# Layer two's queries and keys: one product per quarter batch, spread to row groups through device memory

## The reference, cut to what matters

```python
Q = split_heads(X @ W_q.T)
K = split_heads(X @ W_k.T)
Q1, Q2 = (Q[..., :dh], Q[..., dh:])
K1, K2 = (K[..., :dh], K[..., dh:])
A1 = jnp.einsum('bhqd,bhkd->bhqk', Q1, K1) * scaling
A2 = jnp.einsum('bhqd,bhkd->bhqk', Q2, K2) * scaling
attn = jax.nn.softmax(A1, -1) - lam * jax.nn.softmax(A2, -1)
```

## Time and profile before

| what | value |
|---|---|
| median of 3 runs | 1149.87 us (1148.67 to 1150.07) |
| the profiled execution's own time | 1149.82 us |
| its span in the trace | 1148.1 us |
| PE busy | 915.2 us, 80% |
| DVE busy | 842.1 us, 73% |
| ACT busy | 578.9 us, 50% |
| POOL busy | 435.1 us, 38% |
| layer two in the span | from 461.4 to 1148.1 |

### The profile page before, as it was taken

How to read it: one execution, slowest core, us unless ns; L and a number is a source line. 1 busy time by engine, 2 the same in 40 slices (tenths; PEclk the granted TensorE clock), 3 DMA queues, 4 the chain that set the end, 5 groups by cost and what they waited for, 6 DMA issues and landing times.

```text
span 1148.1 us, 17547 instructions
## 1 busy us (share of the span) xinstructions
PE 915.2 (80%) x5805; PEld 564.9 (49%) x5805; DVE 842.1 (73%) x1990; ACT 578.9 (50%) x1401; POOL 435.1 (38%) x623
## 2 busy tenths in 40 slices
PE   7643086797697998888788888888999998987793
PEld 5322034444344556554343453344566665665692
DVE  4587989969999934587667767778677888835674
ACT  4535244354345343455554455544667765684372
POOL 0302353453283514123435224434532427833422
PEclk9867596898799999999988898999999999999797
DMA  7500000001000000100000000002145503462473
GB/s 205 180 0 1 1 0 1 1 0 42 1 1 1 1 1 1 56 1 1 2 1 1 1 1 1 1 1 97 57 125 157 161 17 106 123 203 61 148 247 101
DMA packets 54314, 60.41 MB, mean 53 GB/s; under 512 B 6208, under 2 KB 40656, under 8 KB 54224
## 3 DMA queue, kind: packets, MB, share of 16 engines
q1 hardware_dynamic: 52176, 55.10, 15.8%
q0 software_dynamic: 2048, 4.20, 1.3%
HBM read 46.05 MB, written 13.24 MB: 52 GB/s over the span
## 4 chain that ended last, share of the span: by engine, by line
PE 33%; DVE 11%; ACT 6%; issue 4%; POOL 3%; DMA 1%; POOLq 0%; ACTq 0%; SPq 0%; DVEq 0%
PE banks L857 8%; PE banks L1018 5%; PE banks L933 4%; DVE MX L1532 3%; PE banks L951 3%; PE banks L992 2%; POOL oms L2037 2%; PE banks L888 2%; ACT PT L1852 2%; PE banks L958 1%; ACT yh L1784 1%; PE banks L899 1%; PE banks L1005 1%; PE banks L1030 1%; DVE sil L1481 1%
## 5 line engine op out<-in xcount | busy, mean ns | idle before, releaser
L1532 DVE TENSOR_REDUCE MX<-banks 128x4 f32<-128x512 f32 (+2 forms) x192 | 199.4, 1043 | 51.4 <-PE banks L992 50.8
L1852 ACT ACTIVATE PT<-banks 128x768 f32<-128x768 f32 (+1 forms) x192 | 168.0, 879 | 88.3 <-PE banks L951 87.8
L2014 POOL TENSOR_SCALAR_AFFINE_SELECT PT<-PT 128x256 f32<-128x256 f32 x256 | 105.5, 428 | 174.0 <-ACT PT L1852 173.6
L1737 ACT ACTIVATE T<-Sb,GM 128x32 f32<-128x32 f32 x128 | 45.2, 353 | 122.8 <-DVE Sb L1407 122.6
L958 PE MATMUL banks<-KS,QS 32*128 32x512 f32 (+3 forms) x512 | 90.4, 399 | 13.2 <-DVE MX L1532 11.4
L1018 PE MATMUL banks<-PT,VA 128*17 128x512 f32 (+3 forms) x1024 | 91.8, 455 | 9.0 <-POOL PT L2014 5.3
L951 PE MATMUL banks<-QS,KS 32*128 32x128 f32 (+3 forms) x512 | 90.7, 397 | 8.6 <-ACT PT L1852 5.8
L857 PE MATMUL banks<-xgT,wg 128*128 128x128 f32 x616 | 84.2, 280 | 11.6 <-ACT ysb L1810 11.2
L923 PE MATMUL banks<-w,hid 128*128 128x128 f32 x448 | 68.1, 297 | 27.3 <-DVE hid L1477 21.4
L923 PEld LDWEIGHTS banks<-w,hid 128*128 128x128 f32 x448 | 61.5, 205 | 56.5 <-DVE hid L1477 37.9
L857 PEld LDWEIGHTS banks<-xgT,wg 128*128 128x128 f32 x616 | 74.6, 191 | 21.0 <-issue 19.8
(11 more groups left out here) (282 smaller groups left out, 2115.1 us busy)
## 6 DMA issues: line engine op xcount, KB each, us to landing
wg<-in_ffn_dram SPq DMA_DIRECT2D x77, 386.0 KB, 3.7
yb<-ysb SPq DMA_DIRECT2D x17, 256.0 KB, 3.8
xg<-xs SPq DMA_DIRECT2D x16, 256.0 KB, 3.5
w<-in_ffn_w_dram SPq DMA_DIRECT2D x12, 256.0 KB, 5.7
xs<-zt SPq DMA_DIRECT2D x2, 1472.0 KB, 14.4
xs<-zt SPq DMA_DIRECT2D x1, 1984.0 KB, 13.4
x<-in_L_attn_x_dram SPq DMA_DIRECT2D x4, 256.0 KB, 5.0
out_dram<-x SPq DMA_DIRECT2D x16, 64.0 KB, 1.6
```

The source lines that it names most:

```text
L1532: v_mx.at(e.tensor_reduce(MX[n % 2][:, u:u + nm, qb % 2, 2 * pair:2 * pair + 2, 24].rearrange("p s i -> p i s"), p4, AX.X, ALU.max, negate ...
L1852: a_p.at(e.activation(PT[q % 3][:, 2 * pair:2 * pair + 2, :], where["score", q, pair][:, :, 0:n], ACT.Exp, scale=ISQ8))
L2014: ins = e.affine_select(out=pt, in_=pt, compare_op=ALU.is_ge, fill=0.0, base=0, pattern=[[0, 2], [1, 128]], channel_multiplier=-1)
```

## The change

A quarter has one `qk_in` in place of four. Its product has 128 distinct rows, 64 of queries and 64 of keys (weights `wqk1`). ACT copies it, rounded, to `HR`; DVE writes the low part, product minus `HR`, to `LO`. A new job `divide` on SP writes five pieces of `HR` and `LO` to a DRAM buffer `parts` of 512 rows by 2 KB, so that every row stands where the score products want it, and a job `gather` waits for these writes and loads 256 rows into two tiles of `QS` and 256 into two of `KS`. A fourth row group (zeros, and ones for the keys) is written once, from `c_one`. There are two buffers `parts`, and two of `HR` and `LO`. PE waits for the gather instead of `v_qk`. The three constant loads `selq`, `selk`, `kone` are gone. All shift tables, of both layers, have new values; the core of the diff shows two rows of them.

```diff
-            down0=-1.0, down=-0.8, up0=1.5, rows=-0.3, qk_in=0.3, turn=-1.5, v_in=0.2, up=0.3, table=4.0,
+            down0=-1.0, down=-1.1, up0=1.5, rows=-0.3, qk_in=-0.1, turn=-1.5, up=0.3, table=4.0, weigh_0=-0.5,
...
+    SP=dict(moe_x=18.0, keep=-11.0, fetch=-15.0, bring=-5.5, fetch_1=5.5, moe_x_0=-9.0, bring_2=-12.0,
+            keep_2=-4.5, fetch_2=-3.5, bring_1=-9.5, divide=-2.5, gather=-7.0))
...
 def front_table(b):
@@ -132,15 +132,15 @@
     for part in range(4):
         quarter = 4 * b + part
         if quarter < 2:
-            t, step = ((12.0, 1.3), (20.0, 3.0))[quarter]
+            t = (12.0, 16.0)[quarter]
         else:
-            t, step = BEGIN[quarter - 2] - (6 if part == 0 else 10), 7.0 if part == 0 else 8.0
+            t = BEGIN[quarter - 2] - (2 if part == 0 else 6)
         if part == 0:
             if b:
                 table.append((t - 14, ("stat", 0, 4 + b, (1, b))))
             table.append((t - 9, ("norm" if b else "turn_x", 0, 4 + b, (1, b))))
             table += [(t - 2 + 0.5 * g, ("v_in", b, g)) for g in range(4)]
-        table += [(t + step * f, ("qk_in", b, 4 * part + f)) for f in range(4)]
+        table += [(t, ("qk_in", b, part)), (t + 3.0, ("divide", b, part)), (t + 8.0, ("gather", b, part))]
...
-        wq1 = sb("wq1", [128, 1024])
-        wk1 = sb("wk1", [128, 1024])
+        wqk1 = sb("wqk1", [128, 512])
+        LO = [sb(f"LO{i}", [128, 512], F32R) for i in range(2)]
...
+        parts = [nc.dram_tensor(f"parts{i}", (512, 512), F32).ap() for i in range(2)]
+
+
+        d_parts = [Signal(d_wqkv.sem, 16), Signal(d_out0.sem, 32)]
+        d_gather = [Signal(d_mod0.sem, 32), Signal(d_mod1.sem, 32)]
+
+        def divided(quarter):
+
+            return d_parts[quarter % 2], (32, 48)[quarter % 2] + 80 * (quarter // 2 + 1)
+
+        def gathered_in(quarter):
+
+            return d_gather[quarter % 2], 32 + 32 * (quarter // 2 + 1)
...
-            def qk_in(b, f):
-                s, w_ = f // 2, (wq1, wk1)[f % 2]
-                pe.wait_ge(d_qk1, 32)
+            def qk_in(b, part):
+                pe.wait_ge(d_qk1, 16)
                 pe.wait_ge(a_h[0], 5 + b)
-                i, ps = take_single(("qk_in", b, f))
-                p_q.at(e.matmul(ps[:, :], w_[:, 128 * s:128 * s + 128], hTr[0][:, :], start=True, stop=True))
-                busy[i] = [(v_qk, 16 * b + f + 1)]
+                i, ps = take_single(("qk_in", b, part))
+                p_q.at(e.matmul(ps[:, :], wqk1[:, 128 * part:128 * part + 128], hTr[0][:, :], start=True, stop=True))
+                busy[i] = [(v_qk, 4 * b + part + 1)]
...
-                                pe.wait_ge(v_qk, 4 * op[1] + 4)
+                                pe.wait_ge(*gathered_in(op[1]))
...
 
-            def qk_in(b, f):
-                t = 8 * b + f // 2
-                dst, sel = (QS, KS)[f % 2], (selq, selk)[f % 2]
-                v.wait_ge(a_hr, 16 * b + f + 1)
-                v.wait_ge(p_s, 6 * (t - SLOTS + 1))
-                v_qk.at(e.scalar_tensor_tensor(out=dst[:, t % SLOTS, :], in0=HR[f % 2][:, :].bitcast(F32),
-                                               scalar=sel[:, 0:1], in1=where["qk_in", b, f][:, :],
-                                               op0=ALU.mult, op1=ALU.add))
+            def qk_in(b, part):
+                q = 4 * b + part
+                v.wait_ge(a_hr, q + 1)
+                if q > 1:
+                    v.wait_ge(*divided(q - 2))
+                v_qk.at(e.scalar_tensor_tensor(out=LO[q % 2][:, :], in0=HR[q % 2][:, :].bitcast(F32), scalar=-1.0,
+                                               in1=where["qk_in", b, part][:, :], op0=ALU.mult, op1=ALU.add))
...
-            def qk_in(b, f):
-                ps = where["qk_in", b, f]
-                a.wait_ge(p_q, 16 * b + f + 1)
-                a.wait_ge(v_qk, 16 * b + f - 1)
-                if f % 2:
-                    a_hr.at(e.activation(HR[1][:, :], ps[:, :], ACT.Identity, bias=kone[:, 0:1]))
-                else:
-                    a_hr.at(e.activation(HR[0][:, :], ps[:, :], ACT.Copy))
+            def qk_in(b, part):
+                q = 4 * b + part
+                a.wait_ge(p_q, q + 1)
+                if q > 1:
+                    a.wait_ge(*divided(q - 2))
+                a_hr.at(e.activation(HR[q % 2][:, :], where["qk_in", b, part][:, :], ACT.Copy))
...
-            load(wq1[:, :], "wq1", d_qk1)
-            load(wk1[:, :], "wk1", d_qk1)
+            load(wqk1[:, :], "wqk1", d_qk1)
+            for i in range(2):
+                load(parts[i].rearrange("(m j r) t -> m j r t", j=4, r=8)[:, 3, :, :], None, d_parts[i],
+                     I["c_one"])
...
+            def divide(b, part):
+                q = 4 * b + part
+                to = parts[q % 2].rearrange("(m j r) t -> m j r t", j=4, r=8)
+                sp.wait_ge(a_hr, q + 1)
+                sp.wait_ge(v_qk, q + 1)
+                if q > 1:
+                    sp.wait_ge(*gathered_in(q - 2))
+                load(to[:, 0, :, :], None, d_parts[q % 2], HR[q % 2][:, :].bitcast(F32))
+                load(to[0:8, 1, :, :], None, d_parts[q % 2], HR[q % 2][0:64, :].bitcast(F32))
+                load(to[0:8, 2, :, :], None, d_parts[q % 2], LO[q % 2][0:64, :].bitcast(F32))
+                load(to[8:16, 1, :, :], None, d_parts[q % 2], LO[q % 2][64:128, :].bitcast(F32))
+                load(to[8:16, 2, :, :], None, d_parts[q % 2], HR[q % 2][64:128, :].bitcast(F32))
+
+            def gather(b, part):
+                q = 4 * b + part
+                at = 2 * q % SLOTS
+                sp.wait_ge(*divided(q))
+                sp.wait_ge(p_s, 12 * (q - 3))
+                for i, dst in enumerate((QS, KS)):
+                    load(dst[:, at:at + 2, :].bitcast(F32), None, gathered_in(q)[0],
+                         parts[q % 2][256 * i:256 * i + 256, :].rearrange("(u p) t -> p u t", u=2))
+
+            jobs = dict(divide=divide, gather=gather, fetch=fetch, bring=bring, keep=keep, moe_x=moe_x)
...
-    for k in "qk":
-        w = f("L1_attn_W_" + k).reshape(32, 8, 128)
-        r = np.zeros((32, 32, 128), w.dtype)
-        for j in range(3):
-            r[:, 8 * j:8 * j + 8] = w
-        o[f"w{k}1"] = r.reshape(1024, 128).T
+    qk = np.stack([f("L1_attn_W_" + k).reshape(4, 2, 4, 8, 128) for k in "qk"])
+    o["wqk1"] = qk.transpose(5, 1, 0, 2, 3, 4).reshape(128, 512)
...
-    row = np.arange(128) % 32
-    o["c_selq"] = -((row >= 16) & (row < 24)).astype(np.float32)[:, None]
-    o["c_selk"] = ((row == 24) * 1.0 - ((row >= 8) & (row < 16))).astype(np.float32)[:, None]
-    o["c_kone"] = (row == 24).astype(np.float32)[:, None]
+    one = np.zeros((2, 8, 8, 512), np.float32)
+    one[1, :, 0, :] = 1.0
+    o["c_one"] = one.reshape(16, 8, 512)
```

More of the change, by code:

```diff
@@ L115 @@
-    DVE=dict(up0=3.0, top=1.4, top_t=6.3, qk_in=2.0, up=3.0, down=3.0, route=1.0, place=-2.5, w_o=1.4, rms=-1.5,
-             rms_o=2.5, sum=8.4, norm=-2.0, pick=-8.0, moe_x=6.0, stat=-4.1, o_norm=-2.2, blend=-1.5,
-             place_2=1.0, sum_1=6.9, norm_7=0.5, route_7=-3.5, place_3=-6.0, rms_3=0.5, up_3=1.5, stat_4=2.0,
-             route_5=0.5, pick_0=6.5, down_2=-4.5, moe_x_3=8.0, sum_3=4.0, up_11=-0.5, w_o_1=-0.5, up_2=-0.5,
-             qk_in_1=-0.5),
-    ACT=dict(up0=3.0, down0=2.5, score=1.3, qk_in=1.6, v_in=1.0, norm=2.5, turn_x=3.0, up=2.0, rms_t=2.5,
-             route=1.0, gate_t=1.0, table=5.0, keep=-1.4, o_back=0.9, table_0=3.0, route_5=3.0, turn_1=-0.5,
-             rms_t_2=-0.5, norm_6=-1.0, o_back_0=0.3, turn_0=-1.5, table_1=1.9, up_3=2.0, o_back_2=-0.5),
@@ new lines @@
+    DVE=dict(up0=1.5, top=1.1, top_t=6.3, qk_in=1.5, up=2.7, down=6.0, route=0.1, place=-2.5, w_o=1.0, rms=-3.0,
+             rms_o=1.7, sum=3.7, norm=-2.0, pick=-8.0, moe_x=-1.3, stat=-4.5, o_norm=-3.3, blend=0.5,
+             place_2=1.0, sum_1=7.0, norm_7=0.5, route_7=-3.5, place_3=-6.0, rms_3=0.5, up_3=1.5, stat_4=2.0,
+             route_5=0.5, pick_0=6.5, down_2=-4.5, moe_x_3=8.0, sum_3=4.0, up_11=-0.5, w_o_1=-0.5, up_2=-0.5),
+    ACT=dict(up0=3.0, down0=2.5, score=1.3, qk_in=1.0, v_in=1.0, norm=5.0, turn_x=3.0, up=2.0, rms_t=1.5,
+             route=1.0, gate_t=1.0, table=4.5, keep=-1.1, table_0=3.0, route_5=3.0, turn_1=-0.5, rms_t_2=-0.5,
+             norm_6=-1.0, o_back_0=0.5, turn_0=-1.5, table_1=2.0, up_3=2.0, o_back_2=-0.5),
@@ L252 @@
+    POOL=dict(stat=-9.5, stat_x=16.0, down=3.0, down0=2.5, moe_x=3.5, pairs=-2.0, ktd=-12.5, o_pw=-2.5, o_ol=1.8,
+              o_dk=-2.5, o_state=-2.0, length=-4.5, o_gq=-9.0, moe_x_0=10.0, o_gq_2=-10.5, o_ol_1=4.5,
               length_3=7.0, o_state_2=-1.5, stat_2=6.5, o_gq_1=-8.0, ktd_0=12.0, o_pw_2=2.5, o_dk_2=2.0,
@@ L2103, in _ @@
             load(maskf[:, :], "c_mask", d_late)
-            load(selq[:, :], "c_selq", d_late)
-            load(selk[:, :], "c_selk", d_late)
-            load(kone[:, :], "c_kone", d_late)
             load(lq[:, :, :], "lams", d_late)
```

61 lines of the change are left out of this document (28 added, 33 removed).

## The result

The changed kernel takes 1138.16 us (median of four runs, 1133.94 to 1140.66) against 1149.48 for the kernel before beside it: ratio 0.9903, interval [0.9885, 0.9922], 11.3 us faster where 26.6 were forecast.

The account below looks back on a forecast made before the run. PE, busy 85 to 93% in layer two, was taken as having most to do, with query and key products mostly in line. Terms -26.7 + 1.1 - 1 = -26.6 us on 1149.82 gave 1123.2 us, range 1103 to 1143.

Parts of the forecast that it names:

- The orders of layer one: Layer one's new shift table moves a few jobs by one or two places: -1 us, ends -5 and +5.
- The start: Up to 504 us: uncovered first trip through device memory, clock loss, fewer products; +1.1 us, ends -3 and +6.
- 4 to 7: Sign of being right: PE waits 4 to 7 us for a transfer before the first score step.
- the length of the way: At the start, first product to loaded rows, 465.9 to 478.5: some 12 us, making the first score step 3.4 late.
- Behind the start: After 504 us: 0.7 of 38.1 us of chain share of removed products and copies comes off, -26.7, ends -11 and -38.
- L933's share of the chain: Query and key products' part of the wait chain, 462-957 us: 48.3 us; three quarters of it after 504 counted as removable.
- Rival B: More gaps between steps drop PE's clock, half as many falls again, costing 10 us: 1133 us; chance 0.15.
- PEclk in the middle stretches as before: Sign of being right: PE's granted clock in 504-642 and 642-800 stays as it was, 0.94 and 0.92.
- under 0.90 in 504-800: Sign that PE's clock takes the gain: granted clock under 0.90 in these stretches of layer two.
- Rival A: In layer two the steps set the pace and PE's gaps grow, so only -11 comes off: 1139 us; chance 0.16.
- Rival C: Quarters 9 to 15: SP's queue makes expert weights late, 1165 us; chance 0.08 with other waits of its kind.
- Rival D: Products' share comes off in full, and fewer holders of the single bank spare waits: 1108 us; 0.15 with better.

Follow-up runs that it names:

- the short kernels: Kernel before with 48 ACT and 48 DVE copies cut to 64 of 512 columns, without and with 48 products shortened: 0.9906 and 0.9844.
- the two repeats: The changed kernel run again unaltered on two other chips, against the kernel before on each: ratios 0.9876 and 0.9933.
- The short-product run: Kernel before with 48 of 64 query and key products replaced by a shorter bf16 product nobody needs, copies kept, no transfers: ratio 0.9994.
- the run with fillers: Changed kernel plus unread 128x256 products on PE, meant for places where PE waits, 31 us in all: ratio 1.0103.
- the short copies: Kernel before with ACT's and DVE's query and key copies cut to 64 of 512 columns from quarter 4 on, all products kept: ratio 0.9906.

## Why the prediction was wrong

**The orders of layer one, -1 forecast, +6.3 measured.** The step that failed: "DVE is busy for 93.26 of 100 us there, so little can be won", from which I took a small number of either sign. A full engine bounds what can be won, not what can be lost. The ends, -5 and +5, did not hold it, and the exchange of tables shows it to be the table's (3.4 us in the kernel before, some 7 in the changed one). The prediction had named layer one moving by over 5 us as a sign of being wrong. This is the largest of the three misses, 7.3 of 15.6 us. What the trace shows in its place is a scan that ends 2.5 us late and 3.8 us more between its end and the barrier. DVE's wait for POOL's `sn`, 4.0 to 10.5 us, goes with the table but is made up for by other waits. Which job's move did it is open.

**The start, +1.1 forecast, +4.3 measured,** inside its ends. The way was right in every link (product, copy, low part, five writes, landing, loads), 7.42 us of wait lay just outside "4 to 7", and the links were 0.3 to 1 us too short: DVE's `hid` ahead of the low part 1.0, the issues 1.0, the landing 0.5, the loads 0.3. With some 0.6 of smaller differences the first step is 6.8 us late, not 3.4. The issue of a write from SBUF was priced by a load's 0.43 us; it takes 0.64. The other two terms came out together: -4.3 for five fewer products and +2.0 for the clock make -2.3, and from first step to first score product it is -2.5 (28.9 to 26.4). So the step that failed here is the length of the way, +3.4 forecast and +6.8 measured.

**Behind the start, -26.7 forecast, -21.6 measured.** The size is near and the reason was wrong. The sum took 0.7 of L933's share of the chain as what its removal would free. Taking 26 of the products' 41 us away alone freed nothing, and the new way without the new tables brought 17 us, not 26.7. My reading is that the chain named the operation that happened to stand last, in a place where PE, DVE and ACT hand work to and fro. DVE's and ACT's part, which I had listed and then costed only in part (5.8 us), is worth 11 where 22 and 18 us of their work go, the products give some 7 on top of that, and layer two's table, costed at nothing, 4 to 7. These add to 22 to 25 us, against the 21.6 measured; since the short kernels take off less than the change does, that they agree so well is partly luck.

**Rival B, the clock,** is what, as I read it, took the products' worth. I gave it half as many falls again and 10 us. To 1034 us I count 10 falls before and 11 after (13 and 15 in the two repeats), and they are longer: of the 11, six last 10 to 14 us, where all 10 before last 3 to 7. "PEclk in the middle stretches as before" failed, and "under 0.90 in 504-800" came true for 642-800. The Trainium skill, page "TensorE: Matmul & The Clock Gate", section on a second failure mode, says that PE going idle often and briefly loses its clock again and again. The short-product run agrees, by 42.8 to 93.6 us of half-speed time. That the clock is the cause and not a companion is argued, not shown: in the run with fillers it rose again and the time did too, since the fillers themselves had to be run. No run here holds the clock up without adding work.

**Rival A** had 1139 us, and the measured 1138.16 is that number by luck: its sum was -11 behind the start, +1 and -1, and the runs have -21.6, +4.3 and +6.3. Its mechanism is half right. DVE's and ACT's queues do weigh on the pace of the steps, as the short copies show, but these were relieved too, and PE's gaps did not grow: its wait for the maximum is 7.6 us, and from the first to the last score product it is idle for 62.6 us before and 63.4 after. Of the 20.0 us that this stretch is shorter by, all is busy time of PE (466.7 to 445.9). **Rival C** did not happen: expert weights were waited for 0.3 us in all, and 0.2 us even with the transfers doubled. There it was the gathers that became late. **Rival D** did not come off.

## What to carry to other kernels

A share of the chain of waits says where the end was last held, not what removal gives: where three engines alternate, take the work off one alone on the chip before summing it, and don't measure it by doubling, since work added on PE in the changed kernel cost 0.8 of itself and work removed from the kernel before gave 0. A retuned table of orders is a change of its own with its own sign by stage; time it apart, since here layer one's lost 6 us of what the rest won. A wait that grew by just the time that is missing is not yet the cause: follow the stage's own marks behind it, which here had caught up. The first pass of a pipeline through device memory is paid in full, and keeping the old way for it alone was among the best repairs.

## What was unexpected of the hardware

- PE's time at 1.2 GHz rose when its work shrank: 42.8 to 93.6 us for 26 us less work, while its busy time over 530 us stayed at 463 to 467.
- SP's queue takes in most quarters 0.57 to 0.67 us to issue a 128 or 256 KB write from SBUF to a rearranged place in device memory (1.33 and 1.21 us for two at the start, 1.16 and 1.19 later), against 0.36 to 0.47 for a load.
- The same kernel, the one before, takes 1148 to 1149 us on two chips and 1167 to 1171 on three others. A part of it lies behind the last score product: 113 to 116 us in the kernels profiled on the former, 125 to 128 on the latter.
- Transfers of 1.75 MB a quarter cost nothing measurable from quarter 4 on (0.9924 against 0.9933); with 1.5 MB more, PE waited for gathers eight times behind the start, 39.8 us in all.
